# Gathered rows of a mixture-of-experts job transposed by VectorE behind on-chip transfers, in place of TensorE

## The chip, the cores and the metric

The kernel runs on one core of a Trainium2 chip. The metric is the device time of one execution in microseconds. A core has five engines that run side by side and meet only at semaphores: TensorE (PE; its weight loads are listed as PEld), VectorE (DVE), ScalarE (ACT), GpSimd (POOL) and SyncE (SP). Here SP only issues transfers, and POOL issues the indirect ones, besides some arithmetic. All transfers run on the core's 16 DMA engines.

## The reference

1024 tokens of 512 features pass a feed-forward block, an attention block and the same feed-forward block again:

```python
x = x + 0.5 * ffn(layernorm(x))
x = x + attn(layernorm(x))
x = x + 0.5 * ffn(layernorm(x))
```

The feed-forward block chooses 2 of 16 experts for each token and adds a shared expert. Cut to what matters:

```python
gate = two of E=16 experts per token, with their scores
for each expert e:
    h = silu(xt @ w1[e] + b1[e]) * (xt @ w2[e] + b2[e])    # 512 -> 128
    y = y + gate[:, e] * (h @ w3[e] + b3[e])               # 128 -> 512
z = silu(xt @ sw1 + sb1) * (xt @ sw2 + sb2) @ sw3 + sb3
return y + z
```

All of it is fp32. The attention block has 32 heads of 16 features, one key and value head, a causal mask and a bias linear in distance. The change doesn't touch it.

## The kernel before

The feed-forward block is written once and run twice, as pass f = 0 and pass f = 1. Each pass normalizes the tokens, writes them to `xn_dram` in HBM, routes them, and sorts the 2048 pairs of token and expert into jobs: a job is up to 128 rows of one expert. With these inputs there are 19 jobs in each pass, numbered from 0 (`2 * rest + 5` with `rest` = 7, read from `jm` at run time). The shared expert is computed around the jobs, mostly ahead of them.

A job j goes through the engines in this way; `par` is j % 2, and most buffers have two halves.

- POOL, `gather(j)` (L554): an indirect transfer fetches the 128 rows of the job from `xn_dram` to one place of `xg` (2 KB for each partition, one row a partition). It waits until the place is free, which `xgt` tells.
- PE, `turn` (L1544): four transposes of 128x128 put the features of the rows on the partitions, in PSUM.
- ACT, `gather_copy` (L709): copies them to `xgT` in SBUF. ACT, `weights_copy` (L718): copies the expert's two first weights from `w12`, where the weights of all 16 experts lie, to `wj`.
- PE, `up` (L1559): eight products of 128x128 (the profile shows each as two MATMUL rows), into a PSUM bank of `par`. It waits for `xgT`, for `wj` and for the hidden rows of job j - 2.
- ACT, `silu` (L713), then DVE, `gated` (L1096): the hidden rows `hj`.
- PE, `down` (L1566): one product of 128x512 with `w3`, which waits for the hidden rows and for `rows_out(j - 2)`.
- DVE, `rows_out` (L1103): copies the result from PSUM to `ysb`, once the scatter of job j - 2 has landed. POOL, `scatter_known` (L559): an indirect transfer to `y_dram`.

The order of the work on every engine is the order in which the code is written. On PE it is up(j + 1), down(j), then the turn two jobs ahead, and so on; the turns of jobs 0 to 3 are placed by hand ahead of the loop. On POOL the first LEAD = 5 gathers come first, then gather(j) and the scatter of job j - LEAD in turn. A wait blocks everything behind it on its engine. SP issues in pass 0 the normalized rows, then all expert weights (`experts_in`, L322, for `ew1` and `ew2`, and L345 for `ew3`, in groups of four experts) and a small weight of the attention (L348); then it waits until all scatters have landed (L354) and loads y back (L357). The feature of number c * 128 + p lies on partition p, in block c, in the rows and in the weights alike: a weight arrives from HBM in runs of one row, 128 numbers or 512 bytes.

After the last job, its scatter must land in `y_dram` before y is loaded and added to x (L1054).

## Time and profile before

| | us |
|---|---|
| median of 3 runs | 455.72 |
| lowest, highest | 453.3, 458.74 |
| span of the profiled execution | 449.1 |

The span is from the first to the last instruction that the profiler recorded. The page lists no device time of its own for that execution; between its span and the median of the three runs lie 6.6 us. "Busy" excludes instructions that only wait, branch or issue a transfer from SP. Times of rows are microseconds from the start of the span; a mean of one instruction is in ns. A chain of waits is followed back from the last instruction: at each step to what released it.

### The profile page before, as it was taken

What the parts mean: (1) busy time and instruction counts of PE and PEld (TensorE: products, weight loads), DVE (VectorE), ACT (ScalarE), POOL (GpSimd) and SP (SyncE); (2) the same over time, 40 slices, a digit from 0 to 9 for tenths busy, and PEclk for the clock granted to TensorE, in tenths of its full rate; (3) what the DMA queues carried; (4) which work ended last, traced back from release to release, by engine and by line L of the source; (5) the groups of instructions that cost most, each with busy time, mean ns of one, the idle gap of its engine ahead of it and who ended that gap; (6) DMA issues with size and microseconds to landing.
All of it is one profiled execution on the core that took longest, in us unless ns stands there. A gap on an engine that the chain in (4) does not pass through costs nothing.

```text
span 449.1 us, 8313 instructions
## 1 busy us (share of the span) xinstructions
PE 394.0 (88%) x2788; PEld 276.8 (62%) x2789; DVE 270.9 (60%) x695; ACT 174.9 (39%) x292; POOL 162.9 (36%) x230
## 2 busy tenths in 40 slices
PE   0899899999969998879979989979999879999972
PEld 0687578888647666645545555434587558888650
DVE  4579623333378954888885795666539933233357
ACT  1321246566112312166653454553441326665300
POOL 2521326665304842343432242343001054666300
PEclk9999999999999999999999999989999999999998
DMA  7999994534298569113312200010420043444278
GB/s 231 290 376 311 316 320 164 167 94 160 98 358 251 157 153 218 52 41 96 89 57 59 79 23 11 16 34 23 161 95 0 0 142 109 155 131 151 87 275 332
DMA packets 51180, 66.05 MB, mean 147 GB/s; under 512 B 8318, under 2 KB 30502, under 8 KB 51108
## 3 DMA queue, kind: packets, MB, share of 16 engines
q1 hardware_dynamic: 42780, 43.55, 30.7%
q0 software_dynamic: 6368, 19.32, 13.5%
q10 hardware_dynamic: 2000, 2.76, 2.1%
q8 instruction: 18, 0.29, 0.3%
q14 instruction: 14, 0.11, 0.1%
HBM read 46.32 MB, written 19.79 MB: 147 GB/s over the span
## 4 chain that ended last, share of the span: by engine, by line
PE 55%; DVE 21%; DMA 13%; SPq 4%; issue 4%; POOL 1%; ACT 1%; ACTq 0%; DVEq 0%; POOLq 0%
PE ps L1559 15%; PE ps L1566 7%; PE ps L1709 6%; PE ps L1423 5%; PE ps L1544 4%; DVE arena L1199 3%; PE ps L1685 3%; DMA turns<-in_L_ffn_sw_dram 3%; PE ps L1628 3%; DMA q_dram<-arena 3%; SPq L394 2%; PE ps L1657 2%; DMA arena<-xn_dram,arena 2%; DMA x<-_attn_hidden_states_dram 2%; PE ps L1659 2%
## 5 line engine op out<-in xcount | busy, mean ns | idle before, releaser
L1199 DVE TENSOR_REDUCE arena<-ps 128x3 f32<-128x384 f32 x128 | 68.6, 553 | 24.8 <-PE ps L1659 22.5
L1559 PE MATMUL ps<-arena,wj 128*128 128x128 f32 x608 | 74.1, 274 | 0.0
L1559 PEld LDWEIGHTS ps<-arena,wj 128*128 128x128 f32 x608 | 71.0, 192 | 1.0 <-issue 1.0
L806 ACT ACTIVATE arena<-ps 128x768 f32<-128x768 f32 x64 | 51.3, 811 | 52.0 <-PE ps L1673 51.7
L627 POOL TENSOR_SCALAR_AFFINE_SELECT arena<-arena 128x512 f32<-128x512 f32 x64 | 41.1, 642 | 78.8 <-ACT arena L806 78.4
L1096 DVE SCALAR_TENSOR_TENSOR arena<-ps,arena 128x128 f32<-128x128 f32 x38 | 13.3, 351 | 82.3 <-ACT arena L713 80.4
L1423 PE MATMUL ps<-arena,turns 128*128 128x256 f32 x256 | 57.6, 381 | 0.5 <-DMA turns<-in_L_ffn_sw_dram 0.5
L1423 PEld LDWEIGHTS ps<-arena,turns 128*128 128x128 f32 x256 | 48.1, 190 | 8.9 <-issue 2.1
L554 POOL DMA_INDIRECT arena<-xn_dram,arena x34 | 33.3, 979 | 50.7 <-DVE arena L1036 25.2
L559 POOL DMA_INDIRECT y_dram<-arena x38 | 38.5, 1012 | 34.4 <-DVE arena L1103 25.4
L1657 PE MATMUL ps<-cb 128*128 128x256 bf16 x128 | 35.4, 276 | 12.0 <-DVE arena L1199 11.4
L1566 PE MATMUL ps<-w,arena 128*128 x76 | 39.2, 597 | 0.6 <-DVE arena L1096 0.6
L718 ACT COPY wj<-w 128x1024 f32 x38 | 39.6, 1048 | 0.0
L1659 PE MATMUL ps<-arena 116*128 116x256 bf16 x128 | 34.6, 270 | 0.0
L1464 PE MATMUL ps<-turns,arena 128*128 128x512 f32 x64 | 30.3, 595 | 3.9 <-issue 3.9
L709 ACT COPY arena<-ps 128x512 f32<-128x512 f32 x38 | 22.3, 587 | 27.6 <-PE ps L1544 27.6
L1628 PE MATMUL ps<-arena,wj 128*128 128x256 f32 x128 | 31.6, 383 | 1.4 <-ACT arena L761 1.4
L1657 PEld LDWEIGHTS ps<-cb 128*128 128x128 bf16 x128 | 12.4, 97 | 31.3 <-DVE arena L1199 23.1
L667 ACT ACTIVATE arena<-ps,shb 128x256 f32<-128x256 f32 x16 | 7.6, 475 | 58.0 <-PE ps L1423 58.0
L1709 PE MATMUL ps<-turns,arena 128*128 128x512 f32 x64 | 30.0, 604 | 0.0
L1544 PEld LDWEIGHTS ps<-cf,arena 128*128 128x128 f32 x136 | 16.6, 140 | 20.0 <-issue 17.6
L1685 PE MATMUL ps<-arena 128*32 128x128 f32 (+1 forms) x512 | 28.0, 338 | 0.3 <-POOL arena L627 0.2
(198 smaller groups left out, 601.4 us busy)
## 6 DMA issues: line engine op xcount, KB each, us to landing
arena<-y_dram SPq DMA_DIRECT2D x16, 512.0 KB, 7.7
arena<-q_dram SPq DMA_DIRECT2D x36, 128.0 KB, 2.6
xn_dram<-arena SPq DMA_DIRECT2D x16, 256.0 KB, 6.3
w<-in_L_ffn_ew_dram SPq DMA_DIRECT2D x4, 1024.0 KB, 10.5
q_dram<-arena SPq DMA_DIRECT2D x16, 192.0 KB, 2.5
x<-_attn_hidden_states_dram SPq DMA_DIRECT2D x4, 512.0 KB, 6.4
out_dram<-x SPq DMA_DIRECT2D x8, 256.0 KB, 5.4
arena<-arena SPq DMA_DIRECT2D x30, 64.0 KB
```

The source lines that it names most:

```text
L627: pool.affine_select(diagonal, diagonal, [[0, 2], [0, 2], [1, P]], ALU.is_ge, 0.0, base=0, channel_multiplier=-1).then_inc(sem("sel"), 1)
L718: act.copy(wj[:, par].rearrange("p c f -> p (c f)"), w12[:, ds(e, 1)].rearrange("p a c f -> p (a c f)")).then_inc(sem(f"wj{f}"), 1)
L806: act.activation(pr[:, n % 2, pair, :], ps[:, bank:bank + 2, :].rearrange("p a b -> p (a b)")[:, 0:768], ACT.Exp).then_inc(sem("exp"), 1)
L1199: dve.tensor_reduce(m3[:, h:h + 1, :], ps[:, bank, 0:3 * P].rearrange("p (n k) -> p n k", n=3), AX_X, ALU.max).then_inc(sem("s_max"), 1)
L1423: ins = pe.matmul(o, sw12[:, c, cols], xnT[:, 2 * pair:2 * pair + 2, c, :], start=(c == 0), stop=(c == KC - 1))
L1559: ins = pe.matmul(o, wj[:, par, c, n * INTER:(n + 1) * INTER], xgT[:, par, c, :], start=(c == 0), stop=(c == KC - 1))
L1566: pe.matmul(ps[:, PS_Y + par, :], hj[:, par, :], w3[:, ds(e, 1), :], start=True, stop=True).then_inc(sem(f"y{f}"), 1)
L1628: ins = pe.matmul(ps[:, PS_ST + c, 0:SEQ], wq[:, k, c * P:(c + 1) * P], xaT[b % 2][:, k, :], start=(k == 0), stop=(k == KC - 1))
L1657: pe.matmul(o.rearrange("p (n k) -> p n k", k=P)[:, 0:3:2, :], identb, mask, start=True, stop=True)
L1659: pe.matmul(o[:, P:3 * P], qside[0:R_MAX, p, h, P:2 * P], kT[0:R_MAX, b, :], start=False, stop=True, skip_group_check=True).then_inc(sem(" ...
L1685: ins = pe.matmul(o, vv[:, b, k, 1 - n % 2:1 - n % 2 + 2 * HD], pr_blocks(n % 2, h // 2)[:, k * QT:(k + 1) * QT - k, h % 2, :], start=(k = ...
L1709: ins = pe.matmul(ps[:, at_bank(b, t), :], aT[b % 2][:, c, t * P:(t + 1) * P], wo[:, c, :], start=(c == 0), stop=(c == KC - 1))
```

## The change

Four things change, in both passes.

1. The turns of jobs 4 and later leave PE. For these, SP issues four transfers within SBUF per job (`spread`, one for each block of 32 partitions): 128 features of all 128 rows go to 32 partitions of the new buffer `xs`, four rows to a partition. Then DVE transposes the whole job in blocks of 32x32 with one instruction (`turned`, a STREAM_TRANSPOSE of 128x512), straight to `xgT`. ACT's `gather_copy` goes for these jobs too. `xgT` is now signalled by DVE, and `xgc` tells of ACT's copies for jobs 0 to 3.
2. The feature order follows from it: feature 4 * p + c lies on partition p, in block c. So the turns that stay read every fourth number (`xg[:, j, c::KC]`), and `experts_in` loads four rows of a weight to a partition, which is one run of 2 KB. `w12` and `wj` hold a part (`ew1`, `ew2`) at a time, so that `weights_copy` is still a copy of 1024 numbers.
3. `xg` has four places, which lie where `xn` lay, instead of two and two more in `turns2` (`xg_first`), and a gather from job 8 on waits until the rows of job j - 4 have been spread. A spread waits for its gather and, from job 6 on, for the transpose of job j - 2, which frees the half of `xs`.
4. LEAD goes from 5 to 6: one more gather ahead of the first scatter, and six scatters after the last gather.

```diff
@@ -37,10 +37,13 @@
-LEAD = 5
+LEAD = 6
...
+PLACES = 4
+QUADS = 4
+QP = P // QUADS
@@ -133,7 +136,7 @@
-        w12 = sb("w12", [P, E, KC, 2 * INTER])
+        w12 = sb("w12", [P, E, 2, KC * INTER])
@@ -143,13 +146,12 @@
-        xg_first = turns2[:, SHARED // P * DIM:].rearrange("p (c d) -> p c d", d=DIM)
...
-        wj = sb("wj", [P, 2, KC, 2 * INTER])
-        wq = wj[:].rearrange("p a c f -> p (a c f)").rearrange("p (c f) -> p c f", c=KC)
+        wj = sb("wj", [P, 2, 2, KC, INTER])
+        wq = wj[:].rearrange("p a n c f -> p (a n c f)").rearrange("p (c f) -> p c f", c=KC)
@@ -205,7 +207,9 @@
-        xg = view("ffn", [P, 2, DIM])
+        view("ffn", [P, 2, DIM])
+        xg = view("ffn", [P, PLACES, DIM], at=0)
+        xs = view("ffn", [P, 2, QUADS, QP, KC], at=PLACES * DIM)
@@ -319,12 +323,16 @@
         def experts_in(eng, e, part):
...
-            eng.dma_start(w12[:, e:e + EG, :, part * INTER:(part + 1) * INTER].rearrange("p e c f -> p (e c) f"),
-                          w[e:e + EG].rearrange("e (c p) f -> p (e c) f", p=P)).then_inc(sem(f"ew_in{e // EG}"), 16)
+            eng.dma_start(w12[:, e:e + EG, part, :],
+                          w[e:e + EG].rearrange("e (p c) f -> p e (c f)", c=KC)).then_inc(sem(f"ew_in{e // EG}"), 16)
         def k_rows(eng, b):
...
+        def spreads(j):
+            return 16 * QUADS * (j // 2 - PLACES // 2 + 1)
@@ -349,6 +357,23 @@
+            def spread(j):
+                par = j % 2
+                nc.sync.wait_ge(sem(f"xg{f}_{j % PLACES}"), 16 * (j // PLACES + 1))
+                if j >= PLACES + 2:
+                    nc.sync.wait_ge(sem(f"xgT{f}"), j - PLACES - 1)
+                for g in range(QUADS):
+                    nc.sync.dma_start(xs[g * QP:(g + 1) * QP, par].rearrange("p a d c -> p a (d c)"),
+                                      xg[:, j % PLACES, g * P:(g + 1) * P]).then_inc(sem(f"xs{f}_{par}"), 16)
+            for j in range(PLACES, JOBS_LEAST + 1):
+                spread(j)
+            for i in range(JOBS_LEAST // 2 + 1, JOBS // 2 + 1):
+                with nc.sync.If_lt(nc.sync.to_reg(i - 1 - AHEAD), nc.sync.to_reg(rest)):
+                    for j in (2 * i - 1, 2 * i):
+                        spread(j)
@@ -548,10 +573,13 @@
             def gather(j):
-                if j >= 4:
-                    pool.wait_ge(sem(f"xgt{f}"), j - 3 if j < 6 else j - 1)
-                place, n = (xg_first[:, j - 2, :], j) if j in (2, 3) else (xg[:, j % 2, :], j % 2)
-                pool.indirect_dma_start(place, None, xn_dram,
+                left = j - PLACES
+                if 0 <= left < PLACES:
+                    pool.wait_ge(sem(f"xgt{f}"), left + 1)
+                if left >= PLACES:
+                    pool.wait_ge(sem(f"xs{f}_{left % 2}"), spreads(left))
+                n = j % PLACES
+                pool.indirect_dma_start(xg[:, n, :], None, xn_dram,
...
             def scatter(rows, buf, done):
@@ -572,11 +600,11 @@
-            last = [pool.to_reg(2 * rest + k + 1) for k in range(LAST)]
+            last = [pool.to_reg(2 * rest + 2 * AHEAD + 2 - LAST + k) for k in range(LAST)]
...
-                par = k % 2
+                par = (k + 1 + LAST) % 2
@@ -706,7 +734,7 @@
             def gather_copy(j, par):
...
-                act.copy(xgT[:, par].rearrange("p c q -> p (c q)"), ps[:, PS_XT + par, :]).then_inc(sem(f"xgT{f}"), 1)
+                act.copy(xgT[:, par].rearrange("p c q -> p (c q)"), ps[:, PS_XT + par, :]).then_inc(sem(f"xgc{f}"), 1)
@@ -715,7 +743,7 @@
             def weights_copy(j, par, e):
...
-                act.copy(wj[:, par].rearrange("p c f -> p (c f)"), w12[:, ds(e, 1)].rearrange("p a c f -> p (a c f)")).then_inc(sem(f"wj{f}"), 1)
+                act.copy(wj[:, par].rearrange("p n c f -> p (n c f)"), w12[:, ds(e, 1)].rearrange("p a n f -> p (a n f)")).then_inc(sem(f"wj{f}"), 1)
@@ -728,22 +756,22 @@
-            def two_jobs(i):
+            def two_jobs(i, turned=False):
...
-                gather_copy(2 * i + 3, 1)
+                if turned:
+                    gather_copy(2 * i + 3, 1)
...
-                gather_copy(2 * i + 4, 0)
...
+            two_jobs(0, turned=True)
...
-                two_jobs(0)
...
-            with act.Fori(1 - f, rest + 1) as i:
+            with act.Fori(1, rest + 1) as i:
@@ -1112,20 +1140,29 @@
-            dve.tensor_copy(rowl[:], rowu[:, ds(2 * rest, LAST)]).then_inc(sem("rowl"), 1)
+            dve.tensor_copy(rowl[:], rowu[:, ds(2 * rest + 2 * AHEAD + 1 - LAST, LAST)]).then_inc(sem("rowl"), 1)
+            def turned(j, par, landed):
+                dve.wait_ge(sem(f"xs{f}_{par}"), landed)
+                dve.wait_ge(sem(f"gu{f}"), j - 1)
+                dve.transpose(xgT[:, par].rearrange("p c (s a) -> p a c s", a=QUADS), xs[:, par].rearrange("p a d c -> p a c d")).then_inc(sem(f"xgT{f}"), 1)
...
+            turned(4, 0, spreads(4))
...
-            gated(3, 1)
-            rows_out(2, 0)
...
+                turned(2 * i + 5, 1, 16 * QUADS * i + spreads(5))
+                gated(2 * i + 3, 1)
+                rows_out(2 * i + 2, 0)
+                turned(2 * i + 6, 0, 16 * QUADS * i + spreads(6))
...
-                gated(2 * i + 5, 1)
-                rows_out(2 * i + 4, 0)
+            gated(2 * rest + 3, 1)
+            rows_out(2 * rest + 2, 0)
@@ -1535,13 +1572,11 @@
-            def turn(j, par, n):
-                first = type(j) is int and j in (2, 3)
-                pe.wait_ge(sem(f"xg{f}_{j if first else par}"), n)
-                rows = xg_first if first else xg
+            def turn(j, par):
+                pe.wait_ge(sem(f"xg{f}_{j}"), 16)
...
-                    ins = pe.transpose(ps[:, PS_XT + par, c * P:(c + 1) * P], rows[:, par, c * P:(c + 1) * P], ident)
+                    ins = pe.transpose(ps[:, PS_XT + par, c * P:(c + 1) * P], xg[:, j, c::KC], ident)
...
             def expert(j):
@@ -1549,14 +1584,17 @@
             def up(j, par, before=None):
-                pe.wait_ge(sem(f"xgT{f}"), j + 1)
+                if type(j) is int and j < PLACES:
+                    pe.wait_ge(sem(f"xgc{f}"), j + 1)
+                else:
+                    pe.wait_ge(sem(f"xgT{f}"), j + 1 - PLACES)
...
-                        ins = pe.matmul(o, wj[:, par, c, n * INTER:(n + 1) * INTER], xgT[:, par, c, :], start=(c == 0), stop=(c == KC - 1))
+                        ins = pe.matmul(o, wj[:, par, n, c, :], xgT[:, par, c, :], start=(c == 0), stop=(c == KC - 1))
...
             def down(j, par, e, before=None):
@@ -1566,30 +1604,27 @@
-            turn(0, 0, 16)
-            turn(1, 1, 16)
+            turn(0, 0)
+            turn(1, 1)
...
-            turn(2, 0, 16)
+            turn(2, 0)
...
-            turn(3, 1, 16)
+            turn(3, 1)
...
-            turn(4, 0, 32)
...
-                turn(2 * i + 5, 1, 16 * i + 32)
...
-                turn(2 * i + 6, 0, 16 * i + 48)
...
```

On PE, the loop over two jobs (`for i in range(rest)`), in order of issue. Here it stands before: `cf` holds the identity for the transposes (L1544), `wj` the weights of up (L1559), and `w` is `w3` of down (L1566).

```order
L1548 ISA x2
L1541 ISA
L1544 MATMUL ps<-cf,arena 128x128 x4
L1552 REGISTER_ALU
L1555 REGISTER_ALU
L1559 MATMUL ps<-arena,wj 128x128 x8
L1563 REGISTER_ALU
L1565 REGISTER_ALU
L1566 ISA
L1566 MATMUL ps<-w,arena 128x512
```

And the same place after the change:

```order
L1583 ISA x2
L1590 REGISTER_ALU
L1591 REGISTER_ALU
L1593 REGISTER_ALU
L1597 MATMUL ps<-arena,wj 128x128 x8
L1601 REGISTER_ALU
L1603 REGISTER_ALU
L1604 ISA
L1604 MATMUL ps<-w,arena 128x512
```

The four transposes are gone, with nothing in their place; up and down follow each other.

On DVE, in the same loop, one job before (L1096 is `gated`, L1103 `rows_out`):

```order
L1096 ISA
L1096 SCALAR_TENSOR_TENSOR arena<-ps,arena 128x128
L1100 REGISTER_ALU
L1102 ISA
L1103 COPY arena<-ps 128x512
```

And one job after (L1148 is `turned`, L1124 `gated`, L1131 `rows_out`):

```order
L1147 ISA
L1148 STREAM_TRANSPOSE arena<-arena 128x4x128
L1124 ISA
L1124 SCALAR_TENSOR_TENSOR arena<-ps,arena 128x128
L1128 REGISTER_ALU
L1130 ISA
L1131 COPY arena<-ps 128x512
```

The transpose of job j + 2 stands ahead of `gated(j)` and `rows_out(j - 1)`, so both are queued behind its wait for the spread rows.

On SP, ahead of the wait for the scatters, where before nothing stood between L351 and L357, there are now four transfers for each job from job 4 on (here two jobs from job 7, with their waits):

```order
L368 DMA arena<-arena 32x4x128 [waits xgT0,xg0_3]
L368 DMA arena<-arena 32x4x128 x3
L368 DMA arena<-arena 32x4x128 [waits xgT0,xg0_0]
L368 DMA arena<-arena 32x4x128 x3
```

All of them come behind the weight transfers of pass 0 on SP.

## Rows read from the trace of the kernel before

**Rows 1.** The head of the page: span, then busy us and share of each engine.

```profile
span 449.1 us, 8313 instructions
PE 394.0 (88%) x2788; PEld 276.8 (62%) x2789; DVE 270.9 (60%) x695; ACT 174.9 (39%) x292; POOL 162.9 (36%) x230
```

**Rows 2.** The chain of waits: start us, us, what; three places in the two passes.

```profile
52.14 7.10 DMA arena<-xn_dram,arena
...
70.12 0.86 PE ps L1566 x2
71.42 1.79 PE ps L1559 x16
73.21 0.86 PE ps L1566 x2
74.50 1.79 PE ps L1559 x16
...
362.25 3.52 DMA arena<-xn_dram,arena
...
376.81 0.86 PE ps L1566 x2
```

**Rows 3.** Sums by stretch, the two job loops: columns as in the first line.

```profile
core 0: us, PE busy (x) PEld busy (x) DVE busy (x) ACT busy (x) POOL busy (x), PEclk, DMA share, GB/s
59.90:118.20 58.30, 58.02 (x412) 47.80 (x411) 18.97 (x37) 33.59 (x54) 30.89 (x31) 1.00 0.49 162
366.40:423.50 57.10, 57.09 (x409) 47.26 (x407) 17.62 (x36) 33.39 (x54) 31.45 (x32) 1.00 0.41 134
```

**Rows 4.** Groups, 77.5 to 114.1 us: xcount | busy, mean ns | idle before, releaser.

```profile
L559 POOL DMA_INDIRECT y_dram<-arena x12 | 12.2, 1018 | 6.9 <-DVE arena L1103 3.8 <-issue 3.0
L554 POOL DMA_INDIRECT arena<-xn_dram,arena x10 | 9.7, 974 | 7.8 <-PE ps L1544 7.8
L1103 DVE COPY arena<-ps 128x512 f32<-128x512 f32 x12 | 8.3, 692 | 0.0
L709 ACT COPY arena<-ps 128x512 f32<-128x512 f32 x12 | 7.0, 587 | 9.6 <-PE ps L1544 9.6
L1096 DVE SCALAR_TENSOR_TENSOR arena<-ps,arena 128x128 f32<-128x128 f32 x12 | 4.2, 351 | 24.6 <-ACT arena L713 24.6
```

**Rows 5.** Timeline of both passes' starts: start us, us, instruction, idle before.

```profile
58.94 0.94 POOL L554 DMA_INDIRECT arena<-xn_dram,arena  x1 [3.34 <-PE ps L1544]
...
64.85 0.69 DVE L1103 COPY arena<-ps 128x512 f32<-128x512 f32 x1
...
66.36 1.02 POOL L559 DMA_INDIRECT y_dram<-arena  x1 [5.20 <-DVE arena L1103]
...
366.02 0.94 POOL L554 DMA_INDIRECT arena<-xn_dram,arena  x1 [0.30 <-issue]
```

**Rows 6.** Transfers of 64 KB within SBUF, in the attention: SP timeline, then chain.

```profile
202.03 0.53 SPq L445 DMA_DIRECT2D arena<-arena  x1
202.60 0.60 SPq L447 DMA_DIRECT2D arena<-arena  x1
...
222.63 3.12 DMA arena<-arena
...
289.84 1.83 DMA arena<-arena
```

**Rows 7.** Expert weights: two stretches (w1/w2, then w3), and SP's last issue.

```profile
38.20:41.50 3.30, 3.30 (x15) 2.10 (x14) 2.96 (x15) 0.48 (x1) 0.07 (x1) 1.00 1.01 317
41.50:44.20 2.70, 2.70 (x20) 2.44 (x19) 2.49 (x10) 1.07 (x2) 0.00 (x0) 1.00 1.07 343
...
60.14 1.49 SPq L348 DMA_DIRECT2D turns<-in_L_attn_Wqkv_dram  x1
```

**Rows 8.** Two DVE instructions of other lengths: by line, and in the timeline.

```profile
L1034 DVE COPY arena<-ps x2: 193/193/193, 49.2 to 359.4; 128x32 f32<-128x32 f32 x2
...
44.44 2.28 DVE L1026 TENSOR_TENSOR arena<-cf,arena 128x2048 bf16<-128x2048 f32 x1
```

## The prediction

> **What bounds the kernel now.** I read the head of the page first, for the busy shares [rows 1]: TensorE (PE) 394.0 of 449.1 us, the other engines 60% or less. A share is a mean over stages, so I then read the chain of waits, in order of time, through the job loops [rows 2]. There are two of these (pass 0 from 59.9 to 118.2 us, pass 1 from 366.4 to 423.5), of 19 jobs each, and the reader is to see that the chain stays on PE in both, in a pattern that repeats every 3.08 us: 1.79 of the up products (L1559), 0.86 of a down product (L1566), then 0.43 before the next up product (73.21 + 0.86 = 74.07, next start 74.50). That 0.43 is the four transposes of a `turn` (L1544). The sums by stretch say the same: PE is busy 58.02 of 58.30 us in pass 0, 57.09 of 57.10 in pass 1, at the full granted clock (1.00, the 2.4 GHz level) [rows 3]. So PE work taken out of a loop is time gained, until another engine or a round trip needs more than what is left per job.
>
> **What the change removes.** `turn` goes for jobs 4 to 18: 15 of 19 turns in each pass, 30 in all. 30 x 0.43 = 12.9 us of PE in its own saturated stretch. A job then costs 1.79 + 0.86 = 2.65 us on PE. ACT also loses 15 evacuations of 0.587 us per pass (L709) [rows 4], worth nothing because PE hides ACT. The waits on the PE queue stay as many (transposed rows, weights, hidden rows).
>
> **What it adds, per job, against 2.65 us of PE.**
> VectorE (DVE): one 32x32 block transpose of 128x512 fp32. No row shows one. From below, the loop's own 128x512 copy takes 0.69 us (L1103) [rows 4]; from above, each of the 16 blocks as an instruction of its own, 16 x 0.193 = 3.1 us (the 128x32 copy, L1034) [rows 8]. I take 0.69, since long DVE instructions pay by elements (2048 of them take 2.28 us, L1026 [rows 8], 1.1 ns each). DVE per job: 0.69 + 0.35 + 0.69 (L1096, L1103) + 3 x 0.05 of starts = 1.9 us, below 2.65. The transpose of job j stands ahead of `gated(j - 2)`, and down(j - 2) is needed only 0.86 + 1.79 = 2.65 us after up(j - 2) ends; 0.69 + 0.35 + gaps is 1.2, so it is hidden. The Trainium skill, page "VectorE: DVE Perf Modes", section "The three transpose paths", gives 311 ns for 128x128 in bf16; scaled by 1.1 ns for 384 more elements that would be an estimate of 0.73 us, and the sum would not move; no run so far shows it.
> SyncE (SP): four transfers of 64 KB within SBUF. The kernel has such transfers: issued one behind the other they start 0.57 us apart (202.03, 202.60), and land 1.83 us after issue, 3.12 at worst [rows 6]. So SP works 4 x 0.57 = 2.3 us per job, below 2.65, and rows are spread 3 x 0.57 + 1.83 = 3.5 us after the gather has landed.
> GpSimd (POOL): nothing new, but less time for it: scatter 1.02, gather 0.97 [rows 4] and 0.30 in front of each, 2.6 us. It fits by 0.05.
> DMA engines: 0.41 of pass 1 is busy with 512 KB per job [rows 3], 1.3 us of 3.08. 256 KB more at the same rate is 0.65: 1.9 of 2.65, a share of 0.73. They fit, with longer queues.
>
> **The round trip.** Now a loop over engines closes: the gather of job k + 7 is queued behind the scatter of job k, which waits for `rows_out(k)`; its transpose stands in front of `rows_out(k + 4)`. From one rows_out to the other: 0.82 until the scatter starts (64.85 + 0.69 = 65.54, start 66.36) [rows 5], 1.02 + 0.30, the gather's landing, 3.5 of spreading, 0.69 + 0.35 + 0.69 on DVE and 0.3 of starts. The gather lands 3.52 us after issue in a burst [rows 2]; a lone one in the loop must be shorter, and I take 3.0. Sum 10.7, against 4 x 2.65 = 10.6. That is a tie; since the first jobs are fetched ahead, and rows may be about 1 us late before down(j - 2) is, I cost it at nothing. With 3.52 the sum is 11.2, 2.8 us per job, which would give back 0.15 x 10 jobs x 2 = 3 us. This is the thinnest place.
>
> **The starts.** Pass 1: the gather of job 4 is issued at 366.02 [rows 5], lands by 369.5, is spread by 373.1 and transposed by 373.8, ahead of `gated(2)`, which down(2) needs at 376.81 - 0.43 = 376.4 [rows 2]: no cost. Pass 0: issued at 58.94 [rows 5], and if it takes the 7.10 us of the first gathers there [rows 2], it lands at 66.0, is spread at 69.6 and `gated(2)` ends at 70.7; down(2) would start at 70.12 - 0.43 = 69.69: 1.0 us late, and a second one may follow. SP is free by then: its last weight issue ends at 60.14 + 1.49 = 61.63 [rows 7]. Against it stands the new weight layout: 8.4 MB now come in runs of 512 bytes, afterwards 2 KB, as `w3` already does. Runs of 512 bytes went at 317 GB/s, the `w3` load at 343 [rows 7]: 26.5 against 24.5 us, so the DMA engines are through 2 us earlier and the gather is in less of a crowd. I take 0.5 us of loss (0 to 2). The earlier weights gain nothing else, as ACT waits for none in the chain.
> Small: the eight turns that stay read every fourth element. I take 0; at half speed it would be 8 x 0.43 = 3.4 us. The copy of weights moves as many elements, from one contiguous run to another: 0. Behind the loops everything (last scatter, loads of y, output) hangs on the loop's end and only shifts.
>
> **Sum.** 449.1 - 12.9 + 0.5 = 436.7 us of span. The page gives no device time of its own for this execution; the three runs have a median of 455.72, 6.6 above the span, which I keep: 443.3 us, 2.7% less. The runs lie between 453.3 and 458.74, so about 1% is what can be told from no change.
>
> **Rivals.**
> A, the round trip decides. If spreading lands as the slow row does (3.12) and the gather takes 3.52, because the DMA engines are at three quarters, the sum is 10.7 + 0.5 + 1.3 = 12.5, or 3.1 us per job: the old pace, and only the jobs fetched ahead keep their 0.43 (some two per pass, 1.7 us). 449.1 - 1.7 + 6.6 = 454.0. For it: POOL, SP and DMA all come close to 2.65. Against: the fetches run far ahead and the two worst rows would have to be the rule.
> B, slower: the DVE transpose sets the pace. It decides once it costs over 3.08 - 1.2 = 1.9 us, at a place where it stands ahead of `gated`, so down waits and PE with it. At a quarter of the rate of a copy, 2.28 us, DVE needs 3.47 us per job, 0.39 more than now: x 13 x 2 = 10 us, 465.7. For it: fp32 blocks through strided reads and writes are shown by no row. Against: all DVE rows of 512 elements take 0.69 or less.
> C, GpSimd is held up. Its 2.6 us leave no room; if it had to wait 0.69 us per job beside the transpose, it would need 3.3 us, 0.21 more than now, x 12 x 2 = 5: 460.7. The Trainium skill, page "SBUF — State Buffer", section "Who interferes with whom", says that some VectorE instructions lock GpSimd out of a shared port pair for their whole length, but not one with a single SBUF input outside the two-port modes; the transpose has one input, and the page's list of instructions that take the pair doesn't name it, so by that rule C is unlikely. No row of before shows the two side by side.
>
> **Chances.** Forecast 0.76 (its own range 439.5 to 449.5: all terms at their best and 1% of noise, or the 3 us of the trip, 2 of the start and some of the turns); A 0.13, B 0.06, C 0.05. Faster by over 1% is the forecast and a little of A, 0.78; within 1% the rest of A, 0.11; slower 0.11. The range is 439.5 to 451.5.
>
> **What would show it.** Right: a job period of 2.65 us in the chain with only L1597 and L1604 (up and down) on it, PE busy throughout, a transpose near 0.7 us, DMA share near 0.7 in the loop. A: PE idle in the loop, its wait or DVE's ended by "DMA arena<-arena", period 2.8 to 3.1. B: a STREAM_TRANSPOSE of 2 us or more with DVE full. C: DMA_INDIRECT longer than 1.02 us. Wrong altogether: a PE period that stays at 3.08 with none of these.

## The result, and the profile after

The changed kernel is slower: 467.22 us (median of 4 runs, 462.55 to 468.87) against 454.51 us (4 runs, 449.81 to 458.74), a ratio of 1.028, 95% interval 1.020 to 1.036. The forecast was 443.3 us. Here and below, ratios leave out the few executions that show a slower state of the chip, so a ratio can differ a little from that of the two medians. The profiled execution has a span of 467.1 us; its device time, 468.87 us, is 1.8 above that, so the 6.6 us that the forecast put around the span of before were mostly its distance to the median.

The head of the page after, which answers to [rows 1]:

```profile
span 467.1 us, 8209 instructions
PE 396.4 (85%) x2668; PEld 269.0 (58%) x2669; DVE 298.0 (64%) x725; ACT 156.7 (34%) x261; POOL 162.9 (35%) x230
```

The sums over the two job loops, which answer to [rows 3]:

```profile
59.00:122.70 63.70, 55.74 (x351) 41.69 (x351) 32.64 (x52) 24.25 (x39) 31.21 (x32) 1.00 0.63 182
384.00:441.50 57.50, 49.34 (x290) 37.00 (x288) 30.42 (x48) 19.85 (x32) 28.06 (x29) 0.94 0.59 177
```

TensorE (PE) was busy for all of its loops before. Now it is busy 55.74 of 63.70 us and 49.34 of 57.50, and in pass 1 the granted clock is 0.94. The turns are gone and the loops are not shorter: from job 4 on a job takes 3.5 us in the mean of pass 0 and 3.7 in pass 1, where it took 3.08 before and 2.65 was forecast. The groups of the middle of pass 0, in the stretch of [rows 4], show who waits:

```profile
L1597 PE MATMUL ps<-arena,wj 128*128 128x128 f32 x165 | 21.0, 279 | 1.5 <-issue 0.7 <-ACT wj L746 0.7
L1148 DVE STREAM_TRANSPOSE arena<-arena 128x512 f32<-128x512 f32 x11 | 12.6, 1144 | 17.3 <-DMA arena<-arena 8.2 <-PE ps L1597 3.6 <-remote 2.7
L1604 PE MATMUL ps<-w,arena 128*128 x20 | 10.9, 625 | 4.9 <-DVE arena L1124 4.7
L587 POOL DMA_INDIRECT y_dram<-arena x10 | 10.2, 1020 | 14.8 <-DVE arena L1131 9.1 <-issue 5.7
L582 POOL DMA_INDIRECT arena<-xn_dram,arena x9 | 8.8, 977 | 2.7 <-issue 2.1 <-DMA arena<-arena 0.6
L741 ACT ACTIVATE arena<-ps,arena 128x128 f32<-128x128 f32 x10 | 3.7, 368 | 22.8 <-PE ps L1597 17.4 <-remote 3.8 <-issue 1.5
```

The reader is to see two things. VectorE's transpose (L1148) waits 8.2 us for the transfers. And ScalarE's silu (L741) waits 17.4 us for TensorE, while TensorE in turn waits for `gated` (L1124): a circle, although none of its instructions has become noticeably longer.

**Late signals.** The row of silu led to the cause. The profile doesn't record when a matmul ends; it works out a modelled end. In the kernel before, silu mostly starts 0.14 us after the modelled end of its job's up products (94.80 and 94.93 in one job). In the kernel after it starts up to 4.5 us behind it, with ScalarE idle. The clearest place is in pass 1 of e4_both (below). From the timelines of PE, ACT and POOL:

```profile
390.52 1.95 PE L1605 MATMUL ps<-arena,wj 128*128 128x128 f32 x16
392.31 1.02 PE L1612 MATMUL ps<-w,arena 128*128 x2
393.17 1.95 PE L1605 MATMUL ps<-arena,wj 128*128 128x128 f32 x16
397.09 1.12 PE L1612 MATMUL ps<-w,arena 128*128 x2 [1.97 <-DVE arena L1125]
...
396.20 0.37 ACT L742 ACTIVATE arena<-ps,arena 128x128 f32<-128x128 f32 x1 [4.71 <-PE ps L1605]
...
388.63 0.97 POOL L583 DMA_INDIRECT arena<-xn_dram,arena  x1 [0.30 <-issue]
389.91 1.02 POOL L588 DMA_INDIRECT y_dram<-arena  x1 [0.30 <-issue]
391.23 0.97 POOL L583 DMA_INDIRECT arena<-xn_dram,arena  x1 [0.30 <-issue]
392.51 1.02 POOL L588 DMA_INDIRECT y_dram<-arena  x1 [0.30 <-issue]
393.83 0.98 POOL L583 DMA_INDIRECT arena<-xn_dram,arena  x1 [0.30 <-issue]
```

The up products of 390.52 end at 392.5; their silu starts at 396.20. In between TensorE went on with a down product and with the next job's up products. The trace's semaphore updates say the same: the signals of these three came at 396.07, 396.12 and 396.28, within 0.21 us, though 2.65 us of modelled work lie between the first and the last. Each instruction that waits is thus waiting for a signal that is still out. Meanwhile GpSimd (POOL) issues indirect DMAs with 0.30 us between them, and the signals come 1.3 us after its last one ends. Below, "lateness" is what silu's start lies beyond the usual 0.14 us behind the modelled end of its up products, summed over those of the 38 jobs at which ScalarE was free: 4.7 us before, 22.2 after. (The recorded expectations call the usual distance 0.30 us, from an end taken 0.16 us earlier, and their sums are up to some 1 us higher. This changes no reading.)

A late signal costs twice. The sums of three stretches of the same run, at this place:

```profile
392.00:395.20 3.20, 3.12 (x23) 2.44 (x21) 0.59 (x1) 0.00 (x0) 2.20 (x3) 1.00 0.81 255
395.20:399.00 3.80, 1.28 (x3) 0.47 (x4) 2.40 (x5) 2.50 (x4) 0.65 (x1) 1.00 0.74 204
399.00:402.40 3.40, 3.40 (x17) 3.40 (x18) 1.41 (x2) 0.00 (x0) 2.48 (x4) 0.50 0.68 185
```

TensorE is busy 1.28 of 3.80 us in the second, then the granted clock is 0.50 (the 1.2 GHz level) for 3.4 us, and the job's up products are slow in it. In the timeline:

```profile
398.84 3.63 PE L1605 MATMUL ps<-arena,wj 128*128 128x128 f32 x16 [0.63 <-issue]
```

3.63 us, where the same row at 390.52, at the 2.4 GHz level, has 1.95.

### The profile page after: what moved, and what is told of

It is laid out like the page before. It is cut to its first block, busy times and chain, and to the rows that moved or that the text cites. A ratio compares the mean times of both kernels' runs of the same rounds, so it can differ in the third digit from the quotient of the medians.

```text
span 467.1 us, 8209 instructions
## 1 busy us (share of the span) xinstructions
PE 396.4 (85%) x2668; PEld 269.0 (58%) x2669; DVE 298.0 (64%) x725; ACT 156.7 (34%) x261; POOL 162.9 (35%) x230
## 4 chain that ended last, share of the span: by engine, by line
PE 40%; DVE 23%; DMA 11%; SPq 10%; issue 9%; ACT 2%; POOL 2%; ACTq 1%; another core or an unknown queue 1%; DVEq 0%; POOLq 0%
PE ps L1597 9%; PE ps L1744 6%; PE ps L1460 5%; SPq L419 5%; PE ps L1604 4%; DMA arena<-arena 4%; SPq L368 3%; DVE arena L1236 3%; DMA q_dram<-arena 2%; PE ps L1720 2%; PE ps L1692 2%; PE ps L1501 2%; DMA x<-_attn_hidden_states_dram 2%; DVE x L1082 2%; PE ps L1448 2%
## 5 line engine op out<-in xcount | busy, mean ns | idle before, releaser
L1597 PEld LDWEIGHTS ps<-arena,wj 128*128 128x128 f32 x608 | 73.9, 196 | 24.9 <-issue 24.2
L1597 PE MATMUL ps<-arena,wj 128*128 128x128 f32 x608 | 77.6, 281 | 3.4 <-issue 1.9
L1148 DVE STREAM_TRANSPOSE arena<-arena 128x512 f32<-128x512 f32 x30 | 34.3, 1144 | 50.3 <-DMA arena<-arena 23.1
L1604 PE MATMUL ps<-w,arena 128*128 x76 | 42.0, 635 | 13.1 <-DVE arena L1124 12.0
L582 POOL DMA_INDIRECT arena<-xn_dram,arena x38 | 37.1, 976 | 41.1 <-DVE arena L1064 25.2
L741 ACT ACTIVATE arena<-ps,arena 128x128 f32<-128x128 f32 x38 | 14.0, 369 | 76.2 <-PE ps L1597 60.4
L1501 PE MATMUL ps<-turns,arena 128*128 128x512 f32 x64 | 33.2, 644 | 4.4 <-issue 4.4
L1744 PE MATMUL ps<-turns,arena 128*128 128x512 f32 x64 | 30.0, 604 | 0.0
L1693 PE MATMUL ps<-arena 116*128 116x128 bf16 x128 | 28.4, 222 | 0.0
```

Source lines behind the costliest of these rows:

```text
L1501: ins = pe.matmul(ps[:, z_bank(t), :], hidden[t // 2 % 2][:, c, t % 2 * P:(t % 2 + 1) * P], sw3s[:, c, :], start=(c == 0), stop=(c == SHAR ...
L1597: ins = pe.matmul(o, wj[:, par, n, c, :], xgT[:, par, c, :], start=(c == 0), stop=(c == KC - 1))
L1604: pe.matmul(ps[:, PS_Y + par, :], hj[:, par, :], w3[:, ds(e, 1), :], start=True, stop=True).then_inc(sem(f"y{f}"), 1)
L1744: ins = pe.matmul(ps[:, at_bank(b, t), :], aT[b % 2][:, c, t * P:(t + 1) * P], wo[:, c, :], start=(c == 0), stop=(c == KC - 1))
```

## The experiments

All are timed beside the kernel before; ratios have 95% intervals. "No turning" or "no gather" leaves that part of the computation out, as the expectation says.

**First theory: buffers and order.** A spread waits for the half of `xs` that the transpose of job j - 2 frees, and the transpose stands ahead of `gated`. e1 is the new weight layout alone in the kernel before (all turns on TensorE, reading every fourth number); e2 moves `turned` behind `gated` and `rows_out`; e3 gives `xs` four parts; e4 does both.

```diff
-        xs = view("ffn", [P, 2, QUADS, QP, KC], at=PLACES * DIM)
+        xs = view("ffn", [P, PARTS, QUADS, QP, KC], at=PLACES * DIM)
...
-                turned(2 * i + 5, 1, 16 * QUADS * i + spreads(5))
                 gated(2 * i + 3, 1)
                 rows_out(2 * i + 2, 0)
+                turned(2 * i + 5)
```

> The kernel before with the weight layout alone: four rows of a weight to a partition (runs of 2 KB), the turns of all 19 jobs on TensorE reading every fourth feature, no spreading. Theory T (the loss comes from the round trip of spreading and transposing inside the job loops) expects the pace of before, 3.08 us per job, and 0 to 2 us less than before in all, from gathers in less of a crowd in pass 0. Rival C (the loss, or the 5 us that are lost outside the loops, comes with the new layout) expects 3 to 12 us more than before.

> The changed kernel, but on VectorE the transpose of job j stands behind gated(j - 2) and rows_out(j - 3) instead of ahead of them. Theory T, part 1 (a transpose that waits for its spread rows holds up gated, and so down and TensorE) expects most of the loss back, but two halves of xs still allow only (1.14 transpose + 1.9 issue + 2.9 landing) / 2 = 3.0 us per job: a pace of 3.0 to 3.1, 452 to 457 us. The rival that only the halves of xs count (part 2) expects no change, 465 to 468. The rival that DMA contention is the cost expects no change either.

> The changed kernel with four parts of xs in place of two, so that the spread of job j waits for the transpose of job j - 4 and no longer of j - 2; VectorE's loop over jobs is written out for this, its order is unchanged. Theory T, part 2 (the halves of xs close a loop of 6.0 us per two jobs) expects a gain; with the transpose still ahead of gated I expect 3.1 to 3.3 us per job and 455 to 462 us. The rival that the order alone matters expects 465 to 468, as does DMA contention.

> Both edits together: transposes behind gated and rows_out, and four parts of xs. Theory T expects the pace of TensorE, 2.65 to 2.8 us per job, 441 to 447 us, under the kernel before. DMA contention as the cause expects over 455 us, with TensorE waiting for rows; the price of the transpose (1.14 us) as the cause expects the same, over 460.

Measured: e1 455.25 us, ratio 1.0035 (0.9997 to 1.0074): the layout and the strided turns cost nothing that can be told. e2 465.35 us, 1.022 (1.017 to 1.027). e3 467.69 us, 1.026 (1.020 to 1.032). e4 462.63 us, 1.012 (1.005 to 1.019): 4.6 us back by the medians, 7 by the ratios, not 20 or more. The theory fell as the whole cause; lateness in e4 is 24.9 us.

**Second question: the transfers or the transposes?** e5 puts the same 120 transfers idly beside the kernel before; e6 transposes contiguously; e7 copies four numbers a partition and leaves the transpose out; e8 leaves the transfers out.

```diff
-                dve.transpose(xgT[:, par].rearrange("p c (s a) -> p a c s", a=QUADS), xs[:, par].rearrange("p a d c -> p a c d"))
+                dve.transpose(xgT[:, par].rearrange("p c q -> p (c q)"), xs[:, par].rearrange("p a d c -> p (a d c)"))
...
-                dve.transpose(xgT[:, par].rearrange("p c (s a) -> p a c s", a=QUADS), xs[:, par].rearrange("p a d c -> p a c d"))
+                dve.tensor_copy(xgT[:, par, 0, 0:4], xs[:, par, 0, 0, :])
...
-                for g in range(QUADS):
-                    nc.sync.dma_start(xs[g * QP:(g + 1) * QP, par].rearrange("p a d c -> p a (d c)"),
-                                      xg[:, j % PLACES, g * P:(g + 1) * P]).then_inc(sem(f"xs{f}_{par}"), 16)
```

> The kernel before with its turns on TensorE, and beside them the four 64 KB on-chip transfers a job that the changed kernel makes (jobs 4 to 18 of both passes, 120 in all), read from the resident w3 and written to a place that nobody reads. What it tells apart is why, in the changed kernel and in the two mended ones, ScalarE's silu of a job starts 1 to 4.6 us behind the modelled end of the job's last up product in some 12 of 38 jobs (0.30 us in all the others), 23 to 26 us in all, where the kernel before shows 5 us of such lateness and never more than 1.3 us at one place. If the transfers hold TensorE's products up (theory D), such late starts of 1 us and more show up here too, and since TensorE has no spare time here they lengthen the time: 462 to 475 us. If it is the transposes on VectorE (theory V), or the chain gather, spread, transpose alone (theory C), nothing here waits for the transfers: 453 to 457 us, and late starts as in the kernel before.

> The changed kernel with the transpose on VectorE from contiguous input to contiguous output: the four 32-wide feature blocks lie in another order, so the features are not in the order of the weights (that is the part of the computation that changes); everything else stays. If the strides (elements 16 bytes apart) are what makes the transpose 1.14 us and not 0.69 us, it is 0.6 to 0.8 us here. Theory V with the strides as the cause: the late starts of silu go and the time falls to 443 to 452 us. Theory D or C: the transpose may be shorter, the late starts stay, and the time is 463 to 467 us.

> The changed kernel with its transfers and all its waits, but of the transpose on VectorE only four elements a partition are copied: the rows of jobs 4 to 18 are not turned. Theory V (the transposes hold TensorE's products up): the late starts of silu are gone and the time is 440 to 448 us. Theory D (the transfers do): late starts of 1 us and more stay, 15 us of them or more, and the time is 458 to 465 us. Theory C (the length of the chain alone, 1.1 us shorter here per job): 455 to 460 us with few late starts.

> The changed kernel with its transposes on VectorE, but without the 120 on-chip transfers: VectorE turns what lies in the place they would fill, so the rows of jobs 4 to 18 are not the gathered ones; the gathers are still made, and wait for the gather and the transpose four jobs back. Theory V: the late starts of silu stay, 15 us or more of them, and the time is 455 to 465 us. Theory D: they are gone, and so is the chain's wait for the spread: 440 to 446 us. Theory C: 441 to 446 us as well, so this run tells V from the other two, and the run without transposes tells D from C.

Measured: e5 458.97 us, 1.012 (1.007 to 1.016), lateness 18.8. e6 464.91 us, 1.026 (1.019 to 1.033), 26.3. e7 466.52 us, 1.022 (1.014 to 1.031), 30.3. e8 461.1 us, 1.012 (1.005 to 1.019), 20.0. Neither part is needed: without the transposes the lateness is there, and without the transfers too. e5 fell between its two expectations: late signals as in theory D, but 4.2 us of time and not 8. In e6 the page's row of the transpose is

```profile
L1148 DVE STREAM_TRANSPOSE arena<-arena 128x512 f32<-128x512 f32 x30 | 21.4, 712 | 56.8 <-PE ps L1597 23.8
```

712 ns, against 1144 with elements 16 bytes apart: the strides cost 0.43 us each, and taking them away gave no time that can be told.

**Third: TensorE itself, or what is left?** e9 leaves out both. e10 and e11 add filling on TensorE to it, in the place of the turns: four transposes (3.08 us a job again), or four products (3.54 us). e12 is e4 with four idle transposes at every second job.

```diff
+            def fill(par):
+                for c in range(KC):
+                    pe.transpose(ps[:, PS_XT + par, c * P:(c + 1) * P], w3[:, 0, c * P:(c + 1) * P], ident)
...
                 e3 = expert(2 * i + 3)
+                fill(1)
                 up(2 * i + 4, 0, 2 * i + 3)
```

> The changed kernel without its 120 on-chip transfers and without its transposes on VectorE (four elements a partition are copied in their place), so the rows of jobs 4 to 18 are not turned at all. The late starts of silu stayed when the transfers alone were taken out (21 us) and when the transposes alone were (31 us). Theory P: they come from TensorE itself, once its job is up and down products alone at 2.65 us a job with no turn between them. Then they stay here, 12 us of them or more, at the same jobs as without the transfers (5 and 12 of both passes), and the time is 452 to 462 us. Theory E: either of the two additions is enough to cause them, so without both they go: 438 to 445 us.

> The kernel of e9_neither with four transposes of constant data on TensorE put back for each of jobs 4 to 18, where the turns stood before; nobody reads what they write. Theory P: the job is 3.08 us again, the late starts fall to the 5 to 8 us that the kernel before shows, and the time is that of the kernel before, 451 to 457 us, no more than in e9_neither or only a little: 12.9 us of work added for nearly nothing. Theory E: 12.9 us is added to a kernel without late starts, the same 451 to 457 us, but then e9_neither has to be at 438 to 445 us. A third possibility is that the late starts stay with the turns back too: then the time is 460 to 472 us, and the cause is something else that the change brought (gathers further ahead, four places, SyncE's waits).

> As e10_fill_t, but the filling is four products of resident weights (128x128 by 128x128, the form of the up products, 0.11 us each) and not transposes, so the pace is the same 3.08 us a job while the share of products in TensorE's work is 100% as in e9_neither. If the pace of the jobs is what matters, the late starts are as rare as in e10_fill_t and the time is 451 to 457 us. If the share of products matters (theory P in its strict form: an unbroken row of products is what is held up, a transpose is a rest), the late starts stay at 15 us or more and the time is 460 to 475 us.

> The kernel of e4_both (transfers, transposes, four parts of the landing place, transposes behind the gated product and the rows out; it computes everything) with four idle transposes on TensorE at every second job from the fifth on. Theory P: the average job is 2.87 us, the late starts of silu fall from 26 us to under 12 us, and the time falls although work is added: 450 to 458 us against the 462.6 us of e4_both. If the late starts don't depend on TensorE's mix of work: they stay, and the time is 463 to 470 us.

Measured: e9 458.52 us, 1.008 (1.004 to 1.012), lateness 23.3. e10 460.28 us, 1.013 (1.009 to 1.018), 17.2. e11 466.62 us, 1.026 (1.022 to 1.030), 0.1. e12 468.09 us, 1.027 (1.022 to 1.032), 30.5. e9 alone fitted the theory that TensorE's unbroken products do it; e10 kept its late signals with the turns' work put back (the third possibility of its expectation). e11, with nothing but products in its loops, has hardly any lateness and a period of 3.54 us in every job there, and e12 got worse (450 to 458 us were expected). So TensorE's mix of work doesn't explain it. But e11 isn't at the pace of e10: each filling product took two rows of 0.11 us, twice what was expected, and its 466.6 us come from that added work. By itself e11 can't tell a slower pace from a cause elsewhere; e14 below can, at the same pace. What differs too is how GpSimd's work lies. e11's timelines of ACT and POOL:

```profile
90.91 0.37 ACT L739 ACTIVATE arena<-ps,arena 128x128 f32<-128x128 f32 x1 [2.24 <-issue]
...
94.45 0.37 ACT L739 ACTIVATE arena<-ps,arena 128x128 f32<-128x128 f32 x1 [2.24 <-issue]
...
89.64 1.02 POOL L585 DMA_INDIRECT y_dram<-arena  x1 [1.14 <-issue]
90.96 0.98 POOL L580 DMA_INDIRECT arena<-xn_dram,arena  x1 [0.30 <-issue]
93.28 1.02 POOL L585 DMA_INDIRECT y_dram<-arena  x1 [1.34 <-DVE arena L1129]
```

Pairs, with over a microsecond between them. In each of the fifteen kernels with more than 12 us of lateness GpSimd has at least one run of four or more in the loops, mostly 0.30 us apart.

**Fourth: GpSimd.** e13 is the changed kernel without the gathers of jobs 6 to 18; e14 is e11 with the gathers of two jobs together and one idle gather between; e15 is e10, and e16 is e4, with a wait for TensorE in front of each gather; e17 is e10 with an earlier such wait; e18 is e4 without those gathers.

```diff
             for j in range(LEAD, JOBS_LEAST + 1):
-                gather(j)
                 scatter_known(j - LEAD)
...
                 elif j % 2:
                     gather(j)
+                    extra((j - LEAD) // 2)
                     gather(j + 1)
...
+                if j >= 2 * PLACES:
+                    pool.wait_ge(sem(f"gu{f}"), j - 3)
...
+                if j >= 2 * PLACES:
+                    pool.wait_ge(sem(f"y{f}"), j - 5)
```

> The changed kernel as it is, with its transfers and its transposes, but without the gathers of jobs 6 to 18 (26 of the 38 gathers; the spreads read rows that lie there), so those jobs compute on other rows. GpSimd's indirect DMA instructions fall from two a job to one, 1.3 us a job. Theory G: what holds TensorE's signals back (late starts of silu, with two or three semaphore updates of TensorE arriving within 0.2 us) is a run of three and more indirect DMA instructions on GpSimd with 0.3 us between them; the kernel before has runs of two, all the kernels with late starts have runs of four and six. Then the late starts go here (under 5 us in all) and the time is 440 to 447 us. Theory P (TensorE's own products at 2.65 us a job, whatever GpSimd does): 15 us or more of late starts stay, and the time is 458 us or more.

> The kernel of e11_fill_m (product filling, 3.54 us a job, 0.2 us of late starts in all) with the gathers of two jobs issued together and one more gather of other rows to an idle place between them, from job 7 on: five gathers more per pass, and runs of four indirect DMA instructions on GpSimd where there were runs of two. TensorE's work is unchanged. Theory G: late starts of 1 us and more come up at these runs, 10 us or more in all, and the time is 470 us or more against the 466.6 us there. Theory P: TensorE is as full as there, no late starts, 465 to 468 us.

> The kernel of e10_fill_t (transposes as filling, 3.08 us a job like the kernel before, 17.8 us of late starts, 460.3 us) with one wait more: from job 8 on the gather of job j waits on GpSimd until the up products of job j-4 are done, as in the kernel before, so that GpSimd's instructions come in pairs, once a job. Nothing else changes. Theory G: the late starts fall to 8 us or less, and the time to 452 to 456 us, by a wait that only delays GpSimd. Theory P: 15 to 20 us of late starts stay, 458 to 462 us.

> The kernel of e4_both (everything computed, no filling) with the same one wait more on GpSimd: the gather of job j, from job 8 on, behind the up products of job j-4. At 2.65 us a job two instructions with their gaps take GpSimd 2.6 us, so its runs can't be kept to two at that pace. Theory G: runs of four get fewer but don't go; the late starts fall from 26 us to 10 to 20 us, and the time is 452 to 461 us. If the wait costs more than it saves, or the spread now comes too late: 462 to 468 us. A time under 450 us would mean that runs of two at any gap are harmless.

> The kernel of e4_both (four parts of the landing place, transposes behind the gated product and the rows out) without the gathers of jobs 6 to 18, as e13_no_gather is the changed kernel without them. There the late starts were gone (0.7 us) and the time was 452.5 us, since a loop of two jobs still took 6.2 us: a DVE transpose first in the loop waits for its transfers and its buffer. If my first theory is right about that remainder, it is cured here: no late starts, a job of 2.65 us, and a time of 440 to 445 us, what was forecast for the change. If it stays at 450 to 453 us, something else sets the 3.1 us a job.

> The kernel of e10_fill_t (3.08 us a job) with the gather of job j, from job 8 on, behind the down products of job j-6, a signal of TensorE that comes at the moment at which the kernel before starts its pair of gather and scatter (e15_tied, with a signal half a job later, kept its late starts, 19.3 us, and its runs were of four). If what keeps the kernel before nearly free of late starts is that its gather waits for a signal of TensorE, so that GpSimd pauses as soon as signals are late, then GpSimd's runs are of two, the late starts fall to 8 us or less and the time is 452 to 456 us. If they stay at 15 us or more with runs of two, the length of the runs isn't what counts.

| run | us | ratio to before | lateness, us | runs of 3 and more on GpSimd |
|---|---|---|---|---|
| before | 454 to 456 | | 4.7 | 0 |
| after | 467.22 | 1.020 to 1.036 | 22.2 | 8 |
| e4_both | 462.63 | 1.005 to 1.019 | 24.9 | 8 |
| e13_no_gather | 452.51 | 0.989 to 0.997 | 0.6 | 0 |
| e14_bursts | 481.13 | 1.049 to 1.060 | 27.7 | 9 |
| e15_tied | 457.24 | 1.001 to 1.011 | 18.5 | 8 |
| e16_both_tied | 460.67 | 1.010 to 1.014 | 15.9 | 5 |
| e17_tied_down | 454.26 | 0.995 to 1.002 | 12.9 | 5 |
| e18_both_no_gather | 441.60 | 0.960 to 0.972 | 0.2 | 0 |

The last column counts, in both loops, runs of three or more of GpSimd's indirect DMAs less than 0.5 us apart. In the 20 kernels that were profiled it sorts them without exception: the five with none (before, e1, e11, e13, e18) have at most one job over 1.0 us late, the fifteen others five to ten. GpSimd's busy share would not sort them: it is 28.0 of 52 us in e10 (66 to 118 us) and 30.89 of 58.30 in the loop of before, 54 and 53%, with 17.2 and 4.7 us of lateness. The sorting alone could be either way round, since late signals also bunch GpSimd's work. e14 gives the direction: TensorE does the same work as in e11, and lateness goes from 0.1 to 27.7 us and the time up by 14.5. Its timelines of PE, ACT and POOL at the worst place:

```profile
403.92 1.95 PE L1611 MATMUL ps<-arena,wj 128*128 128x128 f32 x16
...
407.45 0.50 PE L1611 MATMUL ps<-arena,wj 128*128 128x128 f32 x3
408.31 0.61 PE L1611 MATMUL ps<-arena,wj 128*128 128x128 f32 x4 [0.36 <-issue]
409.74 1.00 PE L1611 MATMUL ps<-arena,wj 128*128 128x128 f32 x5 [0.82 <-issue]
...
411.36 0.37 ACT L751 ACTIVATE arena<-ps,arena 128x128 f32<-128x128 f32 x1 [7.36 <-remote]
...
399.81 1.00 POOL L591 DMA_INDIRECT y_dram<-arena  x1 [2.55 <-DVE arena L1157]
401.12 0.99 POOL L580 DMA_INDIRECT arena<-xn_dram,arena  x1 [0.30 <-issue]
402.41 0.96 POOL L586 DMA_INDIRECT arena<-xn_dram,arena  x1 [0.30 <-issue]
```

This is the first of eight in a row. The products of 403.92 end at 405.9, their silu starts at 411.36, and near the end TensorE itself stutters between matmuls.

e18 confirms the rest. Its row for the loop of pass 0, and GpSimd's timeline in pass 1:

```profile
66.00:118.00 52.00, 51.70 (x326) 40.98 (x325) 35.21 (x52) 20.89 (x34) 18.38 (x19) 1.00 0.48 159
```

```profile
386.73 0.98 POOL L588 DMA_INDIRECT y_dram<-arena  x1 [1.66 <-DVE arena L1130]
389.37 0.98 POOL L588 DMA_INDIRECT y_dram<-arena  x1 [1.66 <-DVE arena L1130]
392.01 0.98 POOL L588 DMA_INDIRECT y_dram<-arena  x1 [1.66 <-DVE arena L1130]
```

TensorE is busy 51.70 of 52.00 us, jobs are 2.64 us apart, and the time is 441.6 us. It has all 120 transfers and all 30 transposes in it, and lies near the forecast's 443.3, but it isn't the forecast's kernel: 26 of the 38 gathers are missing. In e13 the lateness went as expected and the time did not: 452.51 us, where 440 to 447 were expected. The section on the prediction comes back to the rest.

e15 and e17 missed their lateness (8 us or less), and e15 its time (452 to 456 us). Their runs were not the pairs that were aimed at: e15 still had runs of four, e17 runs of three and one of five in pass 0. e17's time came out as expected, at the level of the kernel before; its wait is on a signal that comes as early in the job as the turn's did. e16 computes everything, has less lateness than e4, and is no faster that can be told: ratios of 1.0119 and 1.0122. None of the changed versions that compute everything beats the kernel before. At 2.65 us a job two indirect DMAs with their gaps fill GpSimd, so no order of them leaves it a rest.

## Why the prediction was wrong

**The step that cost most: "GpSimd (POOL): nothing new, but less time for it ... It fits by 0.05."** The arithmetic was right. The instructions last 0.98 and 1.02 us as before (the groups above, [rows 4]). What I costed at nothing was the rest that GpSimd loses: 3.08 less 2.6, some 0.45 us a job. The kernel before keeps it. Late signals came in its place, and they cost in waits and in the clock. Taking the gathers out of the loop gives 467.22 - 452.51 = 14.7 us on the changed kernel, and 462.63 - 441.60 = 21.0 on e4_both (15.8 and 21.0 by the ratios). The gathers' own transfers go with them; that their traffic is the cause is unlikely, since e9 is late with a DMA share of 0.41 in the stretch from 66 to 118 us and e18 isn't with 0.48. The rest isn't all: e10 has the pace of before, 3.08 us, and so the same mean rest, but its gathers wait for no signal of TensorE; it has 17.2 us of lateness and a ratio of 1.013. The kernel before, whose gathers wait for a turn, keeps its work in pairs; how much of that the wait does is open, since e17 with a like wait still had runs of three.

**The second step: the round trip, which "I cost at nothing".** I summed the wrong circle. The one from `rows_out` to `rows_out` has four jobs of room. A shorter one closes over two: a spread waits for the transpose of job j - 2, which frees its half of `xs`. The text on the change names this wait; the sum left it out. In e13, where no signal is late, from the chain of waits and from VectorE's timeline:

```profile
70.48 1.14 DVE arena L1146
71.61 0.02 issue
...
71.67 0.55 SPq L368
...
73.56 0.60 SPq L368
...
76.65 1.15 DVE L1146 STREAM_TRANSPOSE arena<-arena 128x512 f32<-128x512 f32 x1 [2.26 <-issue]
```

Transpose 1.14 (from 70.48), four issues of which the last starts 1.9 us after the first (71.67 to 73.56), 3.1 to the landing and the start of the next transpose of this half (76.65): 6.2 us per two jobs, 3.1 a job here and 3.0 in the mean of both loops, the pace of rival A by another circle than A's. e13 against e18 prices it: 452.51 - 441.60 = 10.9 us (12.3 by the ratios); 3.01 less 2.65 over the 14 last jobs of both passes is an estimate of 10.1. The price holds for the two edits together, four parts of `xs` and the transpose behind `gated`; which of them gives how much was tried only with late signals on top (e2, e3), where neither showed. With late signals on top only 4.6 of the 10.9 show (467.22 - 462.63). The two steps together: 443.3 forecast; 441.6 without both; + 10.9 = 452.5; + 14.7 = 467.2. That this adds up is arithmetic and no test: taken in the other order the same sum reads 21.0 + 4.6.

Of the signs that the prediction named, that of A showed: TensorE idle in the loop and VectorE's wait ended by "DMA arena<-arena" (8.2 us). But the period of 3.5 to 3.7 us lies above its 2.8 to 3.1, and that late signals could exist no rival held.

**Terms that were mis-sized without deciding.** The transpose: 0.69 taken, 1.14 measured. The Trainium skill, page "VectorE: DVE Perf Modes", section "The three transpose paths", led to an estimate of 0.73 us, and e6 measures 0.712 for contiguous operands, so the estimate is near for these; the strides, which neither it nor my sum has, made it 1.144. Rival B is out, since 1.14 is under its 1.9. A spread's transfers: 0.57 us apart taken, some 0.64 measured; landing 1.83 taken, 2.0 to 4.0 on the chains of waits of the kernels here. The DMA share: 0.73 forecast, 0.63 and 0.59 measured, at a slower pace.

**Terms that held.** PE's 0.43 per turn and 2.65 per job (e18's jobs are 2.64 apart). The weight layout and the strided turns: nothing (e1). That TensorE is the bound of before. Rival C as I priced it, a longer GpSimd, didn't happen; here the rule on shared ports and the rows agree. The same section of the Trainium skill ("SBUF — State Buffer", "Who interferes with whom") ends on "PE and ACT never wait on anyone." The section is on the ports of SBUF, and no run here tells whether these have a part in it. Read as a promise that nothing on GpSimd reaches TensorE's timing, the runs don't bear it out: e14 would then have had e11's 0.1 us of lateness, and it has 27.7.

**What stays open.** How GpSimd holds TensorE's signals. The Trainium skill, page "DMA: Bandwidth & Descriptors", section "SWDGE vs HWDGE vs iDMA", says that GpSimd writes the descriptors of its DMAs by software into rings in SBUF, which SyncE's transfers don't use. It agrees with what is seen (SyncE's 120 transfers beside scatters alone, in e13 and e18, are harmless) but no run shows the path. Open too is the threshold: in e10 and e17 the first late signal, 0.6 and 1.4 us late at job 7, comes while runs are still of two, 0.7 to 0.9 us apart. The kernel before has a run of six of its own, the first gathers of pass 1 (360.85 to 368.22 us, outside the loop): the signals of two turns in it are on time, and those near its end are late: up products end at 368.25 and their silu starts at 369.40, 1.0 us late. So a run alone doesn't fix how late signals get. And e5 shows that SyncE's transfers, put beside the pairs of before, bring 18.8 us of lateness where there were 4.7; some of the pairs became runs of three and four, and which came first isn't shown. How much of the 14.7 and the 21.0 us is the gathers' own landing wasn't tried either.

## What to carry to other kernels

When a change shortens the period of the bounding engine, ask of every engine that issues indirect DMAs not only whether it fits, but how much rest it keeps, and which wait spreads that rest: here 0.45 us per pair was nearly harmless where each gather waited for TensorE (4.7 us of lateness) and not where it didn't (e10, 17.2), and with 0.05 left the gathers cost 15 to 21 us. A circle must be drawn for every buffer that a wait guards, the shortest first; the one with two places decided, and the one with four that I summed did not. If a wait is put down to an engine whose instruction had long ended, look at what the other engines issue at that moment, before looking for a slow instruction.

## What the runs showed of the hardware

- TensorE's signals can come 1 to 5.4 us after the modelled end of their matmul, two or three within 0.2 us, while TensorE goes on with its queue. It happens mostly beside indirect DMAs on GpSimd that follow each other at 0.30 us in runs of three and more, and now and then beside pairs; five more of them a pass, in such runs, took a kernel from 466.6 to 481.1 us (e11, e14).
- Each such place costs again through the clock: TensorE idles, the granted clock is 0.50 in the stretch that follows, and a job's up products take 3.63 us there where they take 1.95 (rows of e4_both).
- A block transpose of 128x512 fp32 on VectorE takes 0.712 us with contiguous operands and 1.144 us with elements 16 bytes apart on both sides.
- On-chip transfers of 64 KB from SyncE's queue start 0.60 to 0.65 us apart; where they stand on the chains of waits they land 2.0 (e3) to 4.0 us (e7, e18) after issue.
